# An attention and mixture-of-experts layer on one core: the order of all tasks from tables of single places, and two transposes made 128 columns wide

## The reference

```python
x = layernorm(x + attention(x))      # 16 heads of 8 numbers, causal softmax, output projection
x = layernorm(x + ffn(x))
# ffn: router scores = sigmoid(x @ router_w.T); the best 4 of 8 groups, then the best 8 of 64 experts
#      coef[t, e] = 2.5 * score / sum of the chosen scores, and 0 for the experts not chosen
h = silu(x @ Wg[e]) * (x @ Wu[e]) * coef[:, e]      # 64 numbers for each expert
moe_out = sum over all e of h @ Wd[e]
shared = (silu(x @ SWg) * (x @ SWu)) @ SWd
```

## Time and profile before

| | |
|---|---|
| median of 3 runs | 992.98 us (992.63 to 993.03) |
| the profiled execution | 994.74 us, of which its span is 992.6 us |
| TensorE (PE) busy | 944.1 us, 95% of the span |
| DVE, GpSimd, ACT busy | 763.6, 601.9 and 453.0 us |
| PE share of the chain that ended last | 69%, DVE 20% |

### The profile page before, as it was taken

One profiled execution on the slowest core, in us unless ns is written; L12 is line 12 of the kernel. 1 busy time (PEld: TensorE's weight loads), 2 busy tenths in 40 slices (PEclk: granted clock), 3 DMA queues, 4 the chain that ended last, 5 costly groups with the idle time before them and its releaser, 6 DMA issues.

```text
span 992.6 us, 16009 instructions
## 1 busy us (share of the span) xinstructions
PE 944.1 (95%) x4986; PEld 578.9 (58%) x4998; DVE 763.6 (77%) x2373; ACT 453.0 (46%) x866; POOL 601.9 (61%) x651
## 2 busy tenths in 40 slices
PE   5799989999999999999999999999999999999996
PEld 2244556665666655666566655666566656665663
DVE  4665767789967997789967997789967996478665
ACT  3354435454454445454554454554454545533221
POOL 2532127766676657766676657766576657765553
PEclk8799999999999999999999999999999999999999
DMA  8542044322633344332633254432633222332431
GB/s 290 154 153 60 26 133 165 112 95 83 216 98 121 105 152 146 126 97 84 215 98 120 88 167 140 132 98 78 216 104 120 88 94 97 116 129 72 135 118 62
DMA packets 62675, 121.68 MB, mean 123 GB/s; under 512 B 6528, under 2 KB 34048, under 8 KB 62080
## 3 DMA queue, kind: packets, MB, share of 16 engines
q1 hardware_dynamic: 62592, 120.67, 37.7%
HBM read 98.37 MB, written 22.02 MB: 121 GB/s over the span
## 4 chain that ended last, share of the span: by engine, by line
PE 69%; DVE 20%; issue 4%; DMA 3%; ACT 2%; POOL 1%; SPq 0%; POOLq 0%; DVEq 0%
PE acc L659 10%; PE st L589 6%; PE ob L601 6%; PE sm L571 6%; PE pu L530 5%; PE pg L530 5%; PE pu L532 5%; PE pu L531 5%; PE pg L531 4%; PE pg L532 4%; DVE max_out L961 4%; DVE hid L1029 3%; PE acc L526 3%; DVE hid L1020 2%; PE acc L644 2%
## 5 line engine op out<-in xcount | busy, mean ns | idle before, releaser
L773 POOL TENSOR_TENSOR hid<-hid,coef_b 128x512 f32<-128x512 f32 x240 | 308.8, 1287 | 172.6 <-DVE hid L1029 135.6
L961 DVE CUSTOM_DVE_ANT_0 max_out<-sm,causal_sb 128x128 bf16<-128x128 f32 (+3 forms) x512 | 237.3, 485 | 101.1 <-PE sm L571 99.9
L722 ACT ACTIVATE hid<-pg 128x512 f32<-128x512 f32 x243 | 145.2, 597 | 317.1 <-PE pg L532 316.4
L1020 DVE SCALAR_TENSOR_TENSOR hid<-hid,pg 128x512 f32<-128x512 f32 x243 | 166.3, 684 | 73.8 <-ACT hid L722 73.7
L694 ACT ACTIVATE probs<-st 128x512 f32<-128x512 f32 (+1 forms) x384 | 187.4, 526 | 30.2 <-PE st L589 28.3
L777 POOL TENSOR_TENSOR hid_lo<-hid,hid_hi 128x512 fp32r<-128x512 f32 x112 | 143.7, 1283 | 70.1 <-ACT hid_hi L729 68.9
L1029 DVE TENSOR_TENSOR hid<-hid,pu 128x512 f32<-128x512 f32 x235 | 160.3, 682 | 8.7 <-PE pu L532 5.0
L571 PE MATMUL sm<-k_stack,q_stack 72*128 72x128 bf16 (+3 forms) x512 | 137.8, 310 | 14.4 <-DMA k_stack<-k_rows_dram 10.0
L759 POOL TENSOR_SCALAR_AFFINE_SELECT probs<-probs 128x256 f32<-128x256 f32 x256 | 102.0, 422 | 73.7 <-ACT probs L694 73.2
L530 PE MATMUL pg<-x_hi,wg_hi 128*128 128x512 f32 x240 | 140.7, 586 | 1.5 <-DVE hid L1020 1.3
L659 PE MATMUL acc<-hid,wd_sb 128*128 128x512 f32 x246 | 125.8, 592 | 0.4 <-DVE hid L1038 0.4
(11 more groups left out here) (160 smaller groups left out, 1326.8 us busy)
## 6 DMA issues: line engine op xcount, KB each, us to landing
coef_b<-coef_dram SPq DMA_DIRECT2D x128, 512.0 KB, 3.9
q_rows_dram<-qk_parts SPq DMA_DIRECT2D x24, 384.0 KB, 3.3
k_rows_dram<-qk_parts SPq DMA_DIRECT2D x24, 384.0 KB, 3.6
q_stack<-q_rows_dram SPq DMA_DIRECT2D x64, 144.0 KB
k_stack<-k_rows_dram SPq DMA_DIRECT2D x64, 144.0 KB
xT_sb<-in_xT SPq DMA_DIRECT2D x8, 256.0 KB, 4.0
y<-in_x SPq DMA_DIRECT2D x8, 256.0 KB, 4.2
out<-out_sb SPq DMA_DIRECT2D x8, 256.0 KB, 2.7
```

The source lines that it names most:

```text
L722: act.activation(hid_of(n, i), gate_bank(n, i)[:, :], ACT.Tanh, scale=0.5).then_inc(tanh_done, 1)
L773: pool.tensor_tensor(hid_of(n, i), hid_of(n, i), coef_b[:, half % 2, j, :], ALU.mult)\
L961: last = dve.tensor_tensor_reduce(out=max_out[:, seg.nth(BANK_SM, task) % 2, col:col + wide], in0=sm_of(seg, task)[:, col:col + wide], in1 ...
L1020: dve.scalar_tensor_tensor(hid_of(n, i), hid_of(n, i), 1.0, gate_bank(n, i)[:, :], ALU.add, ALU.mult).then_inc(a_done, 1)
```

## The change

The formulas go. For every task of a batch its own place is written in a table: `FIRST`, `SECOND`, `THIRD` and `STEADY` for the attention of batches 0, 1, 2 and 3 to 7, `EXPERTS_FIRST`, `EXPERTS_SECOND`, `EXPERTS` and `EXPERTS_LAST` for the experts of batches 0, 1, 2 to 6 and 7, `WEIGHTS` for loads and chunks. There is one sort over everything, so the first batches' attention is no list of its own any more. The 3,498 tasks are the same. SyncE's first entries are now: ld0, wld0, wld1, q0, qsplit0, k0, ksplit0, wld2, rs0.0, rs0.1, wld3, rs0.2, rs0.3, wld4, mT0.0, wld5, wld6, ld1, rs0.4. The first `mT` stands right after mx0.11. Since the first `g` comes earlier in the list, 206 matmuls of constants are left of 214.

Two transposes change their form. `max_parts` grows from 32 to 128 columns (the added ones are zero), so `mT` has a stationary operand of 128 columns in place of 32; the copy behind it still takes 32 rows. `coefT` transposes two token tiles of 64 experts at once, 128 columns, so two transposes do the work of four; ACT's copy takes 128 x 256 in place of 64 x 512, and the store to HBM becomes two DMAs with runs of 128 numbers.

The diff, with the tables cut to a few of their lines:

```diff
-HEAD = {'mx': (0.1, 0.43, 0.75), 'st': (0.15, 0.222, 0.7), 'mask': 0.82}
-PACKED_HEAD = {'mx': (0.1, 0.28, 0.75), 'st': (0.179, 0.2, 0.6), 'mask': 0.92}
-GROUP = {'mn': (-0.22, 0.14), 'mT': 0.42, 'pv': 0.05, 'ot': 0.67, 'on': 0.99}
-PACKED_GROUP = {'mn': (-0.22, 0.19), 'mT': 0.42, 'pv': 0.1, 'ot': 0.57, 'on': 1.19}
...
-def attention_places(max_at, st_at, pace, proj_at, stack_at, tail_at, tk_pace, head, group, tail):
...
-STEADY_ARGS = (-55.75, -46.0, 2, -64.5, (-59.15, -52.9, -49.4, -47.4, 0.3), -10.25, 0.27)
-
-PACKED_ARGS = ((5.5, 10.496, 1.05, -3.25, (2.6, 4.3, 7.839, 10.9, 0.55), 27.773, 0.094), (22.25, 27.5, 1.1, 13.708, (22.25, 24.5, 26.1, 28.35, 0.05), 56.25, 0.22))
-STEADY = attention_places(*STEADY_ARGS, HEAD, GROUP, TAIL)
-PACKED = {n: attention_places(*args, PACKED_HEAD, PACKED_GROUP, PACKED_TAIL) for n, args in enumerate(PACKED_ARGS)}
-
...
-def moe_places(n):
...
-def order(first_step, last_step, batches):
...
-def prologue_order():
...
+FIRST = {
+    "ld": (-62.251,),
+    "q": (-55.073,),
+    "qsplit": (-51.205, -50.706,),
+    "k": (-49.975,),
+    "ksplit": (-49.204, -48.08,),
+    "v": (-47.955,),
+    "rs": (-47.377, -47.348, -46.692, -44.686, -39.315, -36.909, -31.357, -29.551,),
...
+    "mT": (-41.659, -38.1, -30.692, -25.322,),
+    "st": (-40.985, -40.837, -40.765, -40.691, -40.668, -40.294, -39.646, -39.464, -39.109, -38.561, -38.334,
...
+STEADY = {
+    "ld": (-85.024,),
+    "q": (-64.276,),
+    "qsplit": (-63.926, -63.598,),
+    "k": (-63.291,),
+    "ksplit": (-63.054, -61.989,),
+    "v": (-62.572,),
...
+    "mn": (-48.023, -47.579, -40.146, -39.641, -32.353, -32.348, -24.015, -23.957,),
+    "mT": (-47.231, -38.862, -31.251, -22.493,),
...
+    "coefT": (0.101,),
+    "c": (0.36, 1.513,),
+}
...
+EXPERTS = {
+    "g": (-0.031, 1.095, 2.144, 3.148, 4.171, 4.814, 6.249, 7.158, 8.129, 9.234, 10.47, 10.732, 11.398, 13.119,
+        13.827, 15.17, 15.869, 16.651, 18.048, 19.097, 20.064, 21.175, 22.507, 22.852, 24.078, 25.391, 26.023,
+        27.101, 27.68, 29.04, 29.975, 30.685, 32.135,),
...
+EXPERTS_LAST = {
+    "g": (-0.183, 0.61, 1.003, 2.048, 2.736, 3.509, 8.501, 11.028, 12.294, 13.584, 15.323, 18.515, 18.619,
...
+WEIGHTS = {
+    "wld": (-56.531, -56.384, -47.421, -46.872, -42.585, -41.341, -40.132, -39.275, -25.529,),
+    "chunk": (-49.604, -47.209, -45.46, -44.958, -41.133, -40.296, -35.179, -34.642, -24.091,),
+}
+
+
+def places_of(table):
+
+    return [(at, kind, i) for kind, ats in table.items()
+            for i, at in (ats.items() if type(ats) is dict else enumerate(ats))]
+
+
+def order():
+
+    out = [(at, kind, 0, i) for at, kind, i in places_of(WEIGHTS)]
+    for n in range(B):
+        experts = EXPERTS_LAST if n == B - 1 else (EXPERTS_FIRST, EXPERTS_SECOND, EXPERTS)[min(n, 2)]
+        for table in ((FIRST, SECOND, THIRD, STEADY)[min(n, 3)], experts):
+            out += [(n * UNITS + at, kind, n, i) for at, kind, i in places_of(table)]
     return [(kind, n, i) for _, kind, n, i in sorted(out, key=lambda x: x[0])]
 
 
@@ -224,7 +405,7 @@
 
 
 
-    ALL = Segment(prologue_order() + order(0, B - 1, range(B)))
+    ALL = Segment(order())
 
     with ExitStack() as ctx:
         def sb(name, shape, dt=F32):
@@ -263,7 +444,7 @@
         v_sb = sb("v_sb", [P, 2, NT, VPAD])
         max_out = sb("max_out", [P, 2, S], BF16)
         row_max = sb("row_max", [P, 2, HG, NT])
-        max_parts = sb("max_parts", [P, MAX_PARTS, HG * NT], BF16)
+        max_parts = sb("max_parts", [P, P // (HG * NT), HG * NT], BF16)
         max_rows = sb("max_rows", [MAX_PARTS * HG * NT, P], BF16)
         probs = sb("probs", [P, HG, HEAD_COLS])
         ev = sb("ev", [P, S])
@@ -278,7 +459,7 @@
         x1 = sb("x1", [P, 2, NT, D])
 
         x1T = sb("x1T", [P, S])
-        coef_T = x1T[0:E, :]
+        coef_T = x1T[:, 0:S // 2]
         th = sb("th", [P, NT, E])
         sfc = sb("sfc", [P, NT * E])
         pair_hi = sb("pair_hi", [P, NT * NG * 4])
@@ -495,9 +676,12 @@
                         sp.dma_start(wd_again, Wd[:, 0:PAIRS // 2 * D]).then_inc(wd_in, 16)
                     if kind == "coefT":
                         after(sp, seg, ob_free, BANK_O, task)
-                        sp.dma_start(coef_dram[par], coef_T[:, :]).then_inc(coef_stored, 16)
+                        for t in range(2):
+                            sp.dma_start(coef_dram[par].rearrange("e (k t q) -> t e k q", t=2, q=P)[t],
+                                         coef_T[t * E:(t + 1) * E, :].rearrange("e (k q) -> e k q", q=P))\
+                                .then_inc(coef_stored, 16)
                     if kind == "c":
-                        after(sp, seg, coef_stored, ("coefT",), ("coefT", n, 0), 16)
+                        after(sp, seg, coef_stored, ("coefT",), ("coefT", n, 0), 16 * 2)
 
                         before = ("h", n, 2 * i - 2) if i >= 2 else ("h", n - 1, UNITS - 3 + 2 * i)
                         after(sp, seg, h_done, ("h",), before)
@@ -574,7 +758,7 @@
                         mm.then_inc(sm_full, 1)
                     if kind == "mT":
                         after(pe, seg, maxparts_done, ("mT",), task)
-                        pe.transpose(sm[0:MAX_PARTS * HG * NT, 0:P // 2].bitcast(BF16),
+                        pe.transpose(sm[:, 0:P // 2].bitcast(BF16),
                                      max_parts[:, :, :].rearrange("p a b -> p (a b)"), id_bf[:, :])\
                             .then_inc(sm_full, 1)
                     if kind == "st":
@@ -620,8 +804,9 @@
                         mm.then_inc(ob_full, 1)
                     if kind == "coefT":
                         after(pe, seg, coef_done, ("coefT",), task)
-                        for t in range(NT):
-                            mm = pe.transpose(ob[0:E, t * P:(t + 1) * P], chosen[:, t, :], id_sb[:, :])
+                        for tt in range(NT // 2):
+                            mm = pe.transpose(ob[:, tt * P:(tt + 1) * P],
+                                              chosen[:, 2 * tt:2 * tt + 2, :].rearrange("p t e -> p (t e)"), id_sb[:, :])
                         mm.then_inc(ob_full, 1)
                     if kind == "g":
                         after(pe, seg, a_done, ("a",), ("a", *one_before(n, i)))
@@ -699,7 +884,7 @@
                     if kind == "x1T":
                         after(act, seg, ob_full, BANK_O, task)
 
-                        after(act, seg, coef_stored, ("coefT",), ("coefT", n - 1, 0), 16)
+                        after(act, seg, coef_stored, ("coefT",), ("coefT", n - 1, 0), 16 * 2)
                         act.activation(x1T[:, :], ob[:, :], ACT.Copy)
 
                         after(act, seg, u_full, ("u",), ("u", n - 2, UNITS - 1))
@@ -710,7 +895,7 @@
                                        scale=0.5).then_inc(ob_free, 1)
                     if kind == "coefT":
                         after(act, seg, ob_full, BANK_O, task)
-                        act.activation(coef_T[:, :], ob[0:E, :], ACT.Copy).then_inc(ob_free, 1)
+                        act.activation(coef_T[:, :], ob[:, 0:S // 2], ACT.Copy).then_inc(ob_free, 1)
                     if kind == "g":
                         after(act, seg, g_full, ("g",), task)
 
@@ -798,6 +983,7 @@
 
             dve.memset(filler[:, :], 1.0).then_inc(filler_done, 1)
             dve.memset(q_stack[64:STACK, :, :], 0.0).then_inc(const_done, 1)
+            dve.memset(max_parts[:, MAX_PARTS:, :], 0.0)
             dve.memset(half_power[:, :], -0.5).then_inc(const_done, 1)
             dve.memset(gs[:, :, NG:NG + TOPG], -BIG)
             dve.memset(g_keep[:, :, TOPG:8], -BIG)
```

More of the change, by code:

```diff
@@ new lines @@
+SECOND = {
+    "ld": (-72.431,),
+    "q": (-71.761,),
+    "qsplit": (-69.767, -69.62,),
+    "k": (-69.341,),
+    "ksplit": (-68.987, -68.461,),
[14 rows of a table added]
+    "mask": (-51.293, -47.529, -46.076, -45.517, -40.832, -35.645, -33.87, -32.974, -24.099, -23.934, -22.722,
+        -22.096, -16.697, -16.691, -15.517, -15.024,),
+    "pv": (-44.902, -32.83, -21.468, -13.176,),
+    "ot": (-42.733, -29.97, -18.4, -11.442,),
+    "on": (-41.026, -24.135, -17.153, -11.43,),
+    "ldtok": (-15.158,),
+    "attT": (-9.71,),
+    "oproj": (-9.318,),
+    "ln": (-9.091, -8.868, -8.802,),
+    "x1": (-8.269, -8.101, -7.735, -7.584,),
+    "x1T": (-6.658,),
+    "router": (-6.093,),
+    "tk": (-5.967, -5.294, -5.088, -4.888, -4.804, -4.613, -4.529, -4.07, -4.024, -3.696, -3.176, -2.903,
+        -2.266, -2.124, -1.994, -1.569, -1.337, -1.043, -0.832, -0.462,),
+    "coefT": (0.602,),
+    "c": (1.97, 3.066,),
+}
@@ new lines @@
+THIRD = {
+    "ld": (-69.126,),
+    "q": (-64.593,),
+    "qsplit": (-64.516, -63.774,),
+    "k": (-63.046,),
+    "ksplit": (-61.851, -59.558,),
[14 rows of a table added]
+    "mask": (-43.8, -40.697, -40.139, -37.962, -35.887, -32.19, -30.751, -30.574, -26.893, -24.812, -23.687,
+        -22.382, -17.542, -15.778, -15.169, -14.246,),
+    "pv": (-37.757, -29.662, -21.453, -13.916,),
```

(57 more changed lines are left out.)

81 lines of the change are left out of this document (17 added, 64 removed), and 141 rows, old and new, of tables (EXPERTS, EXPERTS_FIRST, EXPERTS_LAST, EXPERTS_SECOND).

## The result

The changed kernel takes 965.3 us (median of 4 runs, 962.3 to 966.9), against 993.0 for the kernel before (4 runs on the same chip, 992.6 to 994.1): a ratio of 0.9716, with a 95% interval of 0.9686 to 0.9745, 28 us less. The prediction said 973, in a range of 952 to 990. The profiled execution took 966.8, its span is 965.0.

What follows compares the result with a forecast made beforehand. TensorE, busy 95% of the span, was taken as the bound, with stalls mostly for DVE. Terms -4.8 - 10 - 6 - 2 = -23, taken as 20: 975 us profiled, 973 us for runs; range 952 to 990, the forecast's own 964 to 983.

Steps and rivals of the forecast that it cites:

- work (transposes, constants, mixing): TensorE's matmul work: cheaper transposes and fewer constants, less the cost of finer mixing, -4.8 us, leaving 914 us.
- Stalls in a period: TensorE's waits for DVE between shared units, 3.3 us a period: six periods x 1.6 recovered, -10 us.
- Half recovered: Stalls of a period: chosen between all 3.3 us gone and 3.3 more, giving 1.6 us a period.
- the stall feared before u5: Matmul work ahead of u5 falls from 2.4 to 1.2 us, too short for a `b` of 0.68 behind other DVE work.
- Transposes of maxima and coefficients: On TensorE: 50 gaps of 0.10 us around `mT` go, -5; 16 fewer coefficient transposes of 0.11, -1.7 us.
- The reading of 64 columns: The 64-column coefficient transposes show no gap, so the gap around `mT` was put down to its 32-column width.
- Finer mixing: On TensorE: more uncovered fp32 weight loads, +1.9 us, and more borders from fp32 to bf16, +1.5 us.
- The prologue: Start: stacks of heads 4 and 5 issued ahead of a waiting weight load, `mT` earlier; -6 us, bounds 0 and -12.
- The first `st` before 37: Sign in the profile after: the first `st`, at 39.38 in the old kernel, starts before 37 us.
- The end: From 803.60 on, no attention to mix in; the last `d` gets 2.6 us of matmuls ahead, not 1.7: -2 of 11.
- Only the cheaper matmuls show: Rival: as many stalls are made as are taken away, 988 us; chance 14%.
- DVE's order turns against it: Rival: DVE works strictly in order, so `a` behind a late score maximum makes TensorE wait; slower, 999 us; chance 10%.

Runs made afterwards that it cites:

- finx_spread: Old order with both transposes 128 columns wide, only DVE's four `finx` moved to the new table's places: 994.7 us, 1.0009 of the kernel before.
- order_only: The changed kernel's new tables, with both transposes as they were in the kernel before: 971.0 us, 0.9774 of the kernel before.
- maxima_64: Old order with both transposes changed, but the transpose of maxima 64 columns wide in place of 128: 992.3 us, one run, read for its timeline only.
- coef_earlier: The changed kernel with five of the 14 coefficient loads in each of batches 2 to 6 placed earlier: 963.8 us, 0.9705 of the kernel before.
- start_only: Old order with both transposes 128 wide, new places only for loads, attention of batches 0 to 2, experts of 0 and 1: 989.1 us, 0.9956 of the kernel before.
- mid_only: Old order with both transposes 128 wide, new places only for attention of batches 3 to 7, experts of 2 to 6: 995.1 us, 1.0019 of the kernel before.

## Why the prediction was right, and where not

The forecast's mechanism and sign were right, and the time lies inside its own range of 964 to 983, near its edge; its sum was -23 and 20 was taken, 27.6 was measured. By the distances between starts, with the sum for the work made in the same way as in the prediction (914 us; so the work's -5 is not a measurement of its own, and the stalls are what the span leaves):

| term | said | found |
|---|---|---|
| work (transposes, constants, mixing) | -4.8 | -5 |
| up to the first `g` (the remainder) | -6 | -6 (34 to 28) |
| stalls, six periods up to the `g` of batch 6 | -10 | -13 (3.5 to 1.0; then five of 3.3 to 2.6, 0.5, 0.8, 0.8, 1.3) |
| from the `g` of batch 6 | -2 | -4 (7.6 to 5.3; 3.2 to 1.3) |

- *Stalls in a period.* This term was mis-sized. "Half recovered" was a choice between bounds, 1.6 us a period; in the steady periods it was 2.5, as the waits for DVE all but vanished. The distances that I measured between producer and consumer (u4 from 2.1 to 3.4 us, and so on) held; the stall feared before u5 did not come in the middle, and before the first `mT` 0.24 us is left of 0.65 (in batches 4 to 7: 0.48 between the start of the matmul before it and its own, in place of 0.235). The fear was not empty, though: in `finx_spread`, where only part of the new order is there, u5 does wait 1.3. The first new period, to the `g` of batch 2, is 111.0 in this profile only; the four other kernels with this start and middle, but for a few moved loads, and both transposes wide have 109.4 to 109.8 there.
- *Transposes of maxima and coefficients.* -6.7 was said for the two (-5 and -1.7). In the new order the width is worth 5.7 by runs and 6.0 by the starts around the transposes. The fp32 load behind `mT` (18 of 32 transposes now stand ahead of one, 1 before) takes nothing from this: it is uncovered in `order_only` too, and the width saves 0.22 to 0.25 us at these places. The exceptions are the first `mT` of batches 4 to 7, where DVE comes last and 0.02 to 0.04 is saved. That the time depends on the order, 2.6 in the old one, the prediction did not have: it counted cheaper matmuls as a gain wherever they stand, while in the old order some of them stand inside distances at whose end DVE is late. Nor did it have that the new order with 32 columns would make 126 borders of width, where the old one has 114: part of what the width gives in the new order is what the order had added.
- *The reading of 64 columns was wrong.* From the fp32 coefficient transposes I took "no gap at 64 columns" for a rule of widths. `maxima_64` shows the gap at 64 columns for the bf16 transpose. The Trainium skill, TensorEngine Tiling (Array Packing), section Tiling Modes, says that a change of mode drains the engine. For this operand the trace agrees (0.33 and 0.18); for the fp32 ones of the earlier trace rows and of `order_only` it still shows no gap. The matmul ahead is not the reason, as the experiment shows; why the two types differ is open. It did not change the sum, since the change goes to 128.
- *Finer mixing.* +3.4 was said; no run isolates it. The uncovered load was seen behind `mT`.
- *The prologue.* Right in size in this profile, but not by its steps, so the size is in part luck. "The first `st` before 37" failed in the profile of the changed kernel (40.80), though SyncE did issue the stacks early: I took the landing of 4.97 as the price of every pair, and it was 10.6 for the pair before, which had taken up to 8.7 in the old kernel already. In `order_only`, the same start list, it held (36.45), and in `coef_earlier` (37.04) the first `g` stood at 120.7, 4.3 before that of the changed kernel: with an early landing, and 17.1 us at the lower clock in place of 23.9, the start gives about 10, near the bound of 12. So the profile of the changed kernel shows the less lucky case, and its first `g` is still 12.3 earlier than the old one, partly because the new list has less ahead of it (the next stretch, to the shared `g` of batch 1, is 107.0 in place of 105.1).
- *The end.* More than said, 2.3 and 1.9; I have no experiment on the last batch by itself.
- *The rivals.* "Only the cheaper matmuls show" and "DVE's order turns against it" are what the partial orders do: `start_only` 989, `mid_only` 995, `finx_spread` 995, and 1053 with half of the tables. They were real mechanisms, but the dearest two, the stacks behind a coefficient load in SyncE's queue and `pv` behind a late `mask` in GpSimd's list, are not in the prediction, which looked at DVE's order alone.

The other signs came true: L808 (L624 before) x16, 206 weight loads of constants, PE busy 933.0, periods of 109.4 to 111.0, slightly under the 110 to 111 that were said.

## What to carry to other kernels

In a kernel with one common order for all engines, the order is one object: count the stalls at the starts of matmuls, not by idle shares, and judge a new order as a whole, since half of a good one, in the middle batches alone, cost 60 us here (one run each) where the whole gained 22. A matmul made cheaper pays only where its engine isn't waiting for an answer at the end of the stretch: of 4.6 us saved around the transposes 2.6 arrived in the old order, and of 6.0 some 5.7 in the new. Before trying a shift of a few microseconds in a start that waits for DMAs, look at how far the same start varies between executions.

## What the runs showed of the hardware that was not expected

- A transpose with a bf16 stationary operand of 64 columns keeps the gaps of the 32-column one (0.33 us ahead and 0.18 behind in place of 0.235 and 0.053), while the fp32 one of 64 columns has none, behind a bf16 matmul or an fp32 one (0.23 in `order_only`).
- A pair of stacks landed 10.6 us after its issue with four more stack loads and two weight loads issued right behind it, and the first `st` stood at 36.45 or 40.80 in kernels whose start list is the same. The granted clock explains 0.7 us of it; why the landing varies is not known.
- A short operation of DVE waits for GpSimd. The second step of `max_parts`, 128x16, takes 0.17 us (0.13 to 0.18 in the 13 of 32 cases of the changed kernel in which no operation of GpSimd went on for more than 0.06 us after it had started). In the other 19 it takes 0.18 to 1.09 us, and in 18 of them it ends 23 to 33 ns after the GpSimd operation that was running. In the kernel before, 14 of 32 are held in this way, and take 0.40 to 1.22 us; the one ahead of the first `mT` of a batch takes 1.20. In the lines below it ends at 419.03, and the `mT` of the earlier trace rows starts at 419.18. In batches 4 to 7 of the changed kernel the same step takes 0.41, and the stall is 0.24 in place of 0.65. The longer operations of DVE around it (L1206, 0.68 us) run beside GpSimd undisturbed. This is read from the traces; no run moved the GpSimd operation alone. The kernel before, then the changed kernel:

```profile
417.72 1.28 POOL L777 TENSOR_TENSOR hid_lo<-hid,hid_hi 128x512 fp32r<-128x512 f32 x1
417.83 1.20 DVE L978 SCALAR_TENSOR_TENSOR max_parts<-row_max,max_parts 128x16 bf16<-128x16 f32 x1
```
```profile
484.47 1.27 POOL L958 TENSOR_TENSOR hid<-hid,coef_b 128x512 f32<-128x512 f32 x1
484.69 1.09 DVE L1164 SCALAR_TENSOR_TENSOR max_parts<-row_max,max_parts 128x16 bf16<-128x16 f32 x1
```
